# Row maxima of an attention kernel: another spread over the pairs of a block, and another place for one of them on VectorE

## The reference, cut to what matters

```python
# layer 0, on the group-normalised x
q = prelu(conv1x1(x, w1, b1), a1); k = prelu(conv1x1(x, w2, b2), a2)   # 24 channels
v = prelu(conv1x1(x, wa, ba), aa)                                      # 192 channels
score = softmax(einsum('bnc,bcm->bnm', q, k), axis=2)                  # 4096 x 4096 per image
out = einsum('bnm,bmc->bnc', score, v)
x = x + out
# layer 1, on the group-normalised new x, per channel and element
for i in range(4):                      # for xr - 0.5 (lower) and xr + 0.5 (upper)
    logits = einsum('cij,cjn->cin', softplus(m[i]), logits) + b[i]
    if i < 3: logits = logits + tanh(f[i]) * tanh(logits)
x = x + maximum(abs(sigmoid(sign * upper) - sigmoid(sign * lower)), 1e-6)
```

## Time and profile before

| | |
|---|---|
| time, median of 3 runs (lowest to highest) | 4865.89 us (4865.57 to 4873.28) |
| the profiled execution's own time | 4868.1 us |
| its span | 4866.3 us |
| PE busy | 4460.5 us, 92% |
| DVE busy | 4178.8 us, 86% |
| ACT busy | 3717.8 us, 76% |
| POOL busy | 937.5 us, 19% |
| maxima on DVE (L1164) | 1792 times 683 ns |
| maxima on PE (L1438) | 1792 times 380 ns |
| low parts on DVE (L1058) | 1024 times 1316 ns on average |

### The profile page before, as it was taken

The page is one execution under the profiler, slowest core; times in us unless marked ns, Lnnn a source line. Parts: engine busy times, 40 slices in busy tenths (PEclk is TensorE's granted clock), DMA queues, the critical chain, the costliest instruction groups (busy, mean ns, idle before and its releaser), DMA issues.

```text
span 4866.3 us, 107519 instructions
## 1 busy us (share of the span) xinstructions
PE 4460.5 (92%) x38780; PEld 2978.2 (61%) x38780; DVE 4178.8 (86%) x5433; ACT 3717.8 (76%) x4214; POOL 937.5 (19%) x937
## 2 busy tenths in 40 slices
PE   6999989999899998999899998999989999899976
PEld 4888347773477725777257762678617785277821
DVE  6897899978999798996999969899698987989866
ACT  2776887768877697776977769777797777977787
POOL 4200202212122111221112120121202212022112
PEclk9999999999999999999999999999999999999988
DMA  2001421114211142111412023120332113311133
GB/s 66 25 20 30 100 70 47 34 39 105 62 47 40 36 110 51 47 40 46 108 45 57 28 62 98 39 58 27 77 86 60 36 38 73 96 42 34 38 88 95
DMA packets 154989, 279.95 MB, mean 58 GB/s; under 512 B 37441, under 2 KB 37921, under 8 KB 152706
## 3 DMA queue, kind: packets, MB, share of 16 engines
q1 hardware_dynamic: 154434, 272.69, 21.8%
HBM read 205.24 MB, written 50.33 MB: 53 GB/s over the span
## 4 chain that ended last, share of the span: by engine, by line
PE 57%; DVE 17%; issue 13%; ACT 12%; DMA 1%; DVEq 0%; ACTq 0%; SPq 0%; POOL 0%; POOLq 0%
PE ps L1486 10%; PE ps L1488 10%; PE ps L1490 10%; PE ps L1261 7%; DVE mxp L1164 6%; PE ps L1438 6%; ACT th L777 5%; ACT arena L770 5%; DVE arena L1058 4%; PE ps L1360 3%; PE ps L1294 3%; DVE th L1096 3%; PE ps L1346 3%; PE ps L1318 2%; PE ps L1253 1%
## 5 line engine op out<-in xcount | busy, mean ns | idle before, releaser
L1486 PE MATMUL ps<-v_sb,arena 128*128 128x193 f16 x8192 | 2017.5, 246 | 18.4 <-DVE arena L1058 18.4
L1488 PE MATMUL ps<-v_sb,arena 128*128 128x192 f16 x8192 | 2026.6, 247 | 0.0
L1490 PE MATMUL ps<-v_sb,arena 128*128 128x193 f16 x8192 | 2009.6, 245 | 0.0
L732 ACT ACTIVATE arena<-ps 128x1024 f16<-128x1024 f32 x1024 | 1049.9, 1025 | 773.8 <-PE ps L1261 772.8
L1058 DVE TENSOR_TENSOR arena<-arena 128x1024 f16<-128x1024 f32 x1024 | 1346.1, 1316 | 258.4 <-ACT arena L735 258.3
L1164 DVE TENSOR_REDUCE mxp<-ps 128x1 f32<-128x512 f32 x1792 | 1162.2, 683 | 32.5 <-PE ps L1438 24.8
L1096 DVE SCALAR_TENSOR_TENSOR th<-th,gates,ps 128x1024 f32<-128x1024 f32 x768 | 949.9, 1275 | 148.7 <-ACT th L777 141.4
L735 ACT ACTIVATE arena<-ps 128x1024 f32<-128x1024 f32 x1024 | 1046.4, 1022 | 0.2 <-DVE arena L1058 0.2
L1488 PEld LDWEIGHTS ps<-v_sb,arena 128*128 128x128 f16 x8192 | 794.8, 97 | 261.8 <-issue 0.3
L777 ACT ACTIVATE th<-ps,biases 128x1024 f32<-128x1024 f32 x768 | 826.1, 1120 | 119.9 <-PE ps L1346 81.5
L1486 PEld LDWEIGHTS ps<-v_sb,arena 128*128 128x128 f16 x8192 | 792.0, 97 | 150.5 <-issue 28.6
(11 more groups left out here) (147 smaller groups left out, 3448.3 us busy)
## 6 DMA issues: line engine op xcount, KB each, us to landing
x<-x2d SPq DMA_DIRECT2D x1152, 64.0 KB, 2.4
arena<-x2d SPq DMA_DIRECT2D x768, 64.0 KB, 2.5
xp<-x_dram SPq DMA_DIRECT2D x18, 1536.0 KB, 10.1
shared<-x_dram SPq DMA_DIRECT2D x64, 384.0 KB, 3.7
x2d<-shared SPq DMA_DIRECT2D x64, 384.0 KB, 3.0
res<-x2d SPq DMA_DIRECT2D x96, 256.0 KB
out_dram<-res SPq DMA_DIRECT2D x96, 256.0 KB
kst<-shared SPq DMA_DIRECT2D x32, 256.0 KB, 3.3
```

Source lines behind the costliest of these rows:

```text
L732: act.activation(e_hi[:, q % 4, :].rearrange("p (k n) -> p k n", k=2), sc, ACT.Exp)
L1486: pe.matmul(acc, eh, v_sb[:, m, 0:C + 1], start=(m == 0 and t % 2 == 0), stop=False, skip_group_check=True)
L1488: pe.matmul(acc[:, 0:C], eh, v_sb[:, m, VW:VW + C], start=False, stop=False, skip_group_check=True)
L1490: ins = pe.matmul(acc, el, v_sb[:, m, 0:C + 1], start=False, stop=(m == MT - 1), skip_group_check=True)
```

## The change

27 of a block's 32 maxima stay in steps 0 to 10 of the block before, now 2 and 3 in turn (`PER_PAIR`), and the first 5 are taken one block earlier still, in its steps 13 (one), 14 (two) and 15 (two): `EARLY_AT`. This is so for the blocks 2 to 7 of an image, so blocks 0 to 5 do 5 more at their end. Block 0 still takes all 32 of block 1, 4 per step. The two banks swap (`(m + 1) % 2`). A step's last maximum is reduced by DVE in the next step ahead of that step's `low`; what stood behind it in its own step (`logits`, `result`) comes before it. The transposes of the normalised block move to the ends of steps 11 and 12, the additions to steps 12 and 13. New waits: PE in step 0 for the reduction of the 5 early tiles, ahead of the block's first product with v; at the end of step 11 for all 32 maxima; and the early tiles 0 and 1 for the two additions. Tiles 5 and 6 wait for `out_norm`.

```diff
@@ -25,7 +25,9 @@
 LN2 = 0.6931471805599453
 ESHIFT = 14 * LN2
 BIG = 4096.0
-PER_STEP = 3
+EARLY_AT = {13: [0], 14: [1, 2], 15: [3, 4]}
+EARLY = 5
+PER_PAIR = [2, 3, 2, 3, 2, 3, 2, 3, 2, 3, 2]
 START = 1
 
 
@@ -116,8 +118,15 @@
 
 def max_tiles(p, first):
 
-    per, begin = (4, 3) if first else (PER_STEP, 0)
-    return list(range(max(per * (p - begin), 0), min(max(per * (p - begin + 1), 0), MAXES)))
+    if first:
+        return list(range(max(4 * (p - 3), 0), min(max(4 * (p - 2), 0), MAXES)))
+    begin = EARLY + sum(PER_PAIR[:p])
+    return list(range(begin, begin + PER_PAIR[p])) if p < len(PER_PAIR) else []
+
+
+def early_tiles(j, p):
+
+    return EARLY_AT.get(p, []) if j + 2 < BLOCKS else []
 
 
 def tail_unit(i, last):
@@ -1161,7 +1170,7 @@
             def phase_b(b, l):
                 def reduce(base, m, bank):
                     dve.wait_ge(max_mm, base + (m + 1))
-                    dve.tensor_reduce(mxp[:, m // BLOCKS, m % BLOCKS:m % BLOCKS + 1], ps[:, bank + m % 2, :],
+                    dve.tensor_reduce(mxp[:, m // BLOCKS, m % BLOCKS:m % BLOCKS + 1], ps[:, bank + (m + 1) % 2, :],
                                       AX_X, ALU.max).then_inc(max_red, 1)
 
                 for j in range(BLOCKS):
@@ -1176,17 +1185,23 @@
                             denominators(b, j - 1)
                         if p == 12 and not last:
                             rows_out(nxt, free, False)
+
+                        if p >= 1 and not last:
+                            for m in max_tiles(p - 1, first)[-1:]:
+                                reduce(maxes, m, free)
                         if p + 1 < PAIRS or not last:
                             low(pairs, p + 1)
                         if first and l is not None and p == 1:
                             logits(l, UNITS - 1, False)
                         if not last:
-                            for m in max_tiles(p, first):
+                            for m in max_tiles(p, first)[:-1]:
                                 reduce(maxes, m, free)
                             if p == 11:
                                 split_max(nxt, maxes)
-                        if not first and p in (13, 14):
-                            add_half(b, j - 1, p - 13)
+                        if not first and p in (12, 13):
+                            add_half(b, j - 1, p - 12)
+                        for m in early_tiles(j, p):
+                            reduce(dve.compute_val(maxes + MAXES), m, free)
                         if l is not None and p in tails_in(j, RESULT_AT):
                             result(l, tails_in(j, RESULT_AT)[p], False)
                         if last and p == 2:
@@ -1431,11 +1446,12 @@
 
             def phase_b(b, l):
                 def max_tile(base, q_col, m, bank, evacuated):
+
                     if m >= 2:
                         pe.wait_ge(max_red, base + (m - 1))
-                    elif evacuated is not None:
+                    if evacuated is not None and m in (EARLY, EARLY + 1):
                         pe.wait_ge(out_norm, evacuated + START)
-                    pe.matmul(ps[:, bank + m % 2, :], qst[:, q_col + m // BLOCKS * P:q_col + (m // BLOCKS + 1) * P],
+                    pe.matmul(ps[:, bank + (m + 1) % 2, :], qst[:, q_col + m // BLOCKS * P:q_col + (m // BLOCKS + 1) * P],
                               kst[:, (m % BLOCKS) * N:(m % BLOCKS + 1) * N], start=True, stop=True
                               ).then_inc(max_mm, 1)
 
@@ -1461,6 +1477,8 @@
                                 pe.wait_ge(h2_ready, l * SLOTS + SLOTS - 1)
                         if p == 0 and not first:
                             pe.wait_ge(x2_ready, b * 2 * BLOCKS + 2 * (j - 1) + START)
+                            if not last:
+                                pe.wait_ge(max_red, maxes + EARLY)
                         if last and p == 3:
                             pe.wait_ge(out_norm, blocks + START)
                             averages1(b + 1, 0)
@@ -1476,7 +1494,8 @@
                             if p == 3:
                                 pe.wait_ge(lu_ready, l * UNITS + UNITS)
                         todo = max_tiles(p, first) if not last else []
-                        spots = (1, 3, 5, 7) if first else (5, 6, 7) if p == 0 else (2, 5, 7)
+                        spots = (1, 3, 5, 7) if first else (5, 7) if p == 0 else (2, 5, 7) if len(todo) == 3 else (3, 7)
+                        ahead = early_tiles(j, p).copy()
                         for i in range(2):
                             m = 2 * p + i
                             for t in range(NT):
@@ -1493,12 +1512,21 @@
                                     ins.then_inc(summed, 1)
                                 if i * NT + t in spots and todo:
                                     max_tile(maxes, q_next, todo.pop(0), free, None if first else blocks)
-                        if not first and p in (12, 13):
-                            if p == 12:
+                                if i * NT + t in ((6,) if p == 13 else (4, 7)) and ahead:
+                                    if ahead[0] < 2 and first:
+                                        pe.wait_ge(max_rows, blocks + 2)
+                                    elif ahead[0] < 2:
+                                        pe.wait_ge(x2_ready, b * 2 * BLOCKS + 2 * (j - 1) + ahead[0] + 1 + START)
+                                    max_tile(pe.compute_val(maxes + MAXES), q_next + N, ahead.pop(0), free, None)
+                        assert not todo and not ahead
+                        if not first and p in (11, 12):
+                            if p == 11:
                                 pe.wait_ge(out_split, b * (BLOCKS - 1) + j)
+                                if not last:
+                                    pe.wait_ge(max_red, maxes + MAXES)
                             elif not last:
                                 pe.wait_ge(max_rows, blocks + 2)
-                            turn_parts(j - 1, p - 12)
+                            turn_parts(j - 1, p - 11)
 
                 pe.wait_ge(full_ready, pairs + PAIRS)
                 project(0)
```

## The result

The changed kernel takes 4887.69 us (median of 6 runs, 4885.05 to 4890.04), the kernel before 4868.45 beside it (6 runs): ratio 1.0038, 95% interval 1.0027 to 1.0049. It is 19 us slower, between 13 and 24 by the interval; the forecast was 22 slower and 4888 us. The profiled execution took 4885.05 us, its span 4883.3.

The account below looks back on a forecast made before the run. PE was taken to bound the kernel, its idle time being all to win. Per middle block 1.86 us added less 1.65 removed; with block 6 and the first image +22 us, forecast 4888, likeliest range 4876 to 4902, wider 4852 to 4906.

Parts of the forecast that it names:

- PE's idle time bounds the matter, its work is equal: Both profiled blocks: PE bounds them, only its idle time can be won; tiles per block transition stay 32.
- Tile 4, 0.5 us: Block start: PE waits for early tile 4's reduction before going on, 0.5 us in each of 48 block starts.
- The late reciprocals, 0.61 us at tile 5: Pair 0: reciprocals behind reduction and `result` delay ACT's normalising, so tile 5 waits 0.61 us; 0.01 in the first image.
- The low part of step 1 behind POOL's split, +0.5: Pair 1: `low` waits for POOL's split, so the third product stalls 0.55 us where 0.07 was.
- The low part of step 3, +0.2: Pair 3: POOL still first by 0.08 us, `low` waits 0.2 longer, stall 0.87 us.
- What goes: pairs 0, 4 and 8, and 0.46 at the turning: Middle blocks: stalls of 0.24, 0.53 and 0.42 vanish, transposes take 0.46 off at the turning; together 1.65 us per block.
- The sum: Whole kernel: middle blocks 7 us, block 6 of 7 images 10, first image 5; total +22 us.
- The deferral changes nothing by itself: A step's deferred last reduction: order unchanged except step 7's `result`; next `low` starts at most 0.1 us earlier.
- Rival 1: Pair 3: DVE's `low` starts before POOL and the stall goes, -30, total -8, 4858 us; chance 0.14.
- rival 2: Block start: late start hidden, tile 5 and step 1's `low` find all ready; -28, 4838 us; chance 0.12.
- Rival 3: DVE stays behind: four more pairs pay 0.2 us each in 35 blocks, +28, 4916 us; chance 0.11.
- rival 4: Maxima are no bound: gains and losses cancel within 0.2% (9.7 us), 4866; chance 0.10.

Follow-up runs that it names:

- Run 7: Changed kernel with the edits of run 1, run 2 and Run 3, and pair 10's tiles after groups 2 and 5: 4782.8 us, ratio to before 0.9824.
- run 1: Changed kernel with step 15's two early tiles multiplied after groups 2 and 5 instead of 4 and 7: 4865.0 us, ratio to before 0.9992.
- run 2: Changed kernel with step 15's second-layer result taken in the next block's step 0, behind the reciprocals: 4863.2 us, ratio to before 0.9986.
- Run 3: Changed kernel with 2, 2, 3, 2, 2, 3, 3, 3, 2, 3, 2 tiles in steps 0 to 10: 4833.8 us, ratio to before 0.9929.
- run 4: Changed kernel with pair 2's second tile multiplied after group 6 instead of 7: 4859.5 us, ratio to before 0.9981.
- run 5: Kernel before with only the moved transposes and additions, swapped banks and step 11's wait for all maxima: 4854.1 us, ratio 0.9967.
- run 9: Kernel before with the last maximum deferred in all steps but 7, so DVE's order stays as before: 4871.2 us, ratio 1.0004.
- run 6: Kernel before with only each step's last maximum reduced in the next step, ahead of its low part: 4857.7 us, ratio 0.9978.
- run 8: Kernel before with only the two banks of the maxima swapped: 4869.0 us, ratio 1.0002.

## Why the prediction was right

- **PE's idle time bounds the matter, its work is equal.** The second half is right: PE's busy time in the middle block moved by 0.1 us, the block by 0.25. The first half is not, as a size. The middle block's 49.93 - 47.90 is 2.03 us of idle time, and the stalls that I read sum to 3.0. Run 7 has the same tiles in a middle block and takes 47.63, less than PE was busy before, and is itself busy 47.20. So busy time of overlapping matmuls is no floor for a block; the distances between pairs' starts are the better measure, and the forecast went by these.
- **Tile 4, 0.5 us.** Right: the product with v came 0.95 - 0.43 = 0.52 us late; run 1 took it away for 22.7 us, 24 by the forecast's term.
- **The late reciprocals, 0.61 us at tile 5.** Right: 3.10 behind the scores against 3.04 forecast; run 2 took it away for 24.5 us, 26 forecast.
- **The low part of step 1 behind POOL's split, +0.5.** Right: pair 1 went from 3.16 to 3.63, its low part from 1.45 to 1.89 us. **The low part of step 3, +0.2**, by 0.08 us of order: pair 3 went from 3.74 to 3.95, the low part took 2.27. Run 3 took both stalls away (53.9 us for 56), run 4 that of pair 3 (28.2 for 30). That POOL's split is what holds the low part of step 1 is read from its end (1.08 us behind POOL's) and was not varied alone.
- **What goes: pairs 0, 4 and 8, and 0.46 at the turning.** Pairs 4 and 8 take 2.87, as forecast. Pair 0 keeps 0.08 of its 0.24 (2.95 in run 7, 2.87 without a stall), and pair 5 was not squeezed (3.08). The gain of the transposes is shown by run 5, 16.3 us for 16.
- **The sum.** Per block the forecast holds closely: middle blocks +0.2 (measured +0.24, in blocks 4 and 5 +0.3), the seventh +0.33 (+0.38), block 0 +1.08 (+0.97), the first image +5 (+4.2). That makes 23 us for the 22. In the first image two misses cancel: pair 0 came 0.1 longer than forecast and pair 1 0.1 shorter. The two profiled spans differ by 17.0. What the sum left out is the clock at the start of the images: three of them in the profiled execution of before, none after, some 4.5 us; the rest lies in phase A. The medians, 19.2 apart, lie between. The mean granted clock of the six executions after is 0.984, that of all 61 of the kernel before beside the runs 0.982, and within these 61 a clock higher by 0.001 goes with 2.4 us less: by that an estimate of 4 to 5 us, which would make the 23 the 19. The clock was no term of my sum.
- **The level, 4888 for 4887.7, is in part luck.** The kernel before stood at a median of 4865.9 in the three executions that I added 22 to, and at 4868.5 in the six beside the changed one; the difference was 19.
- **The deferral changes nothing by itself.** Right for the order (run 9). My term for its side effect on pair 8, at most 0.1 us in each block, was right too by the trace; but run 6 gained 12.6 us where that makes 4 to 5. A worth of up to 8 us beside it was in none of my terms. Much of it goes with the clock: run 6's ten executions have 0.9835 on the mean and the 15 beside them 0.9816, at 2.4 us for 0.001 an estimate of 4 to 5 us. Its profiled execution has one image start at the half clock, the kernel before three. Why this edit should move the clock, and where the last 2 to 4 us are, stays open.
- **The rivals.** Rival 1 did not happen by its 0.08 us, and run 4 made it happen. Of rival 2, run 2 made the first half happen (tile 5 waits for nothing) and pair 1 still took 3.63: the second half, that the low part of step 1 then finds all ready, does not follow from the first. Rival 3 has nothing for it in the trace (pairs 5, 7 and 9 at 3.08), and rival 4 is excluded by the interval, 13 to 24 us.

## What to carry to other kernels

A spread that is even by count is not what a pipeline of fixed order wants: give the fewer items to the steps in which something else holds the engine (here two to steps 1, 3, 4 and 8), which was worth 54 us against the even spread; that one, with the early tiles, had lost 19. Work taken over a block's border reuses buffers that the next block starts with, so put it early enough in the last step that its consumer is done at the border, and let what the next block waits for (the reciprocals) go ahead of what nobody waits for. Where two engines exclude each other, write down both start times from their releasers: a quarter of a microsecond in one of them was worth 28 us.

## What the runs showed of the hardware that I had not expected

The first pair of phase B takes 4.74 us in some images and 5.8 in others. Below are four windows of the kernel before: 4.4 us ahead of the first products with v of the fourth image, the first 24 of these products, and the same two of the fifth image.

```profile
1866.00:1870.40 4.40, 2.16 (x12) 0.43 (x12) 2.64 (x3) 4.40 (x5) 0.00 (x0) 1.00 1.04 242
1870.57:1873.65 3.08, 3.08 (x25) 2.94 (x25) 2.91 (x3) 1.96 (x3) 0.00 (x0) 0.63 0.81 186
2462.20:2466.60 4.40, 2.16 (x12) 0.43 (x12) 2.64 (x3) 4.40 (x5) 0.00 (x0) 1.00 1.12 276
2466.77:2468.78 2.01, 2.01 (x25) 2.01 (x26) 1.84 (x2) 1.97 (x3) 0.00 (x0) 1.00 0.75 153
```

The granted clock is 0.63 in the second and 1.00 in the fourth, and the timeline of the fourth image shows the fall in its course: the products stand 0.08 us apart and then 0.16.

```profile
1871.23 0.24 PE L1490 MATMUL ps<-v_sb,arena 128*128 128x193 f16 x1
1871.32 0.28 PE L1486 MATMUL ps<-v_sb,arena 128*128 128x193 f16 x1
1871.40 0.36 PE L1488 MATMUL ps<-v_sb,arena 128*128 128x192 f16 x1
1871.55 0.37 PE L1490 MATMUL ps<-v_sb,arena 128*128 128x193 f16 x1
```

That is the lower of the two levels, 1.2 GHz, for a part of the window. Before it PE was busy 2.16 of 4.40 us, with a wait of 2.12 us for DVE just ahead. In the fifth image it was the same, 2.16 of 4.40 and a wait of 2.12, and the clock stayed at 1.00: what PE did just before does not tell the two apart, and no run here shows what does. One such start costs about 1.5 us with the pair behind it (block 0 takes 55.8 for 54.3). Of the seven images 2 to 8, the profiled executions had three such starts before, none after, two in run 1, none in run 2, three in run 3, five in runs 4 and 5, one in run 6, four in run 7, three in run 8 and four in run 9. This is what a change of a few us in this kernel is to be read against; the medians of pairs in middle blocks are not moved by it.
